# A decoder layer on one core: giving the maximum matmuls, turns and P.V places of their own in the written order

## The reference

```python
x = x + self_attention(layernorm(x))        # 16 heads of 16, 512 keys, two masked score entries
x = x + tanh(gate) * (cross_attention(layernorm(x), ctx) @ w_out + b_out)   # 16 heads of 64, 64 keys
h = layernorm(x)
a1, a2 = entmax15(layernorm_noaffine(h @ proj)) @ C1, ... @ C2     # 16 experts, rank 128
h = gelu(((([h, 1] @ Win1) * a1) @ Wout1.T))                       # 1024 wide
x = x + (([h, 1] @ Win2) * a2) @ Wout2.T
```

## Time and profile before

| | |
|---|---|
| median of 3 runs | 1161.67 us (1156.67 to 1162.15) |
| the profiled execution | 1160.25 us, span 1158.4 us |
| TensorE busy | 1042.9 us, 90% |
| VectorE, ScalarE, GpSimd busy | 768.1, 625.3, 150.2 us |
| mean granted clock of TensorE | 0.935 |

### The profile page before, as it was taken

The page is one execution under the profiler, slowest core; times in us unless marked ns, Lnnn a source line. Parts: engine busy times, 40 slices in busy tenths (PEclk is TensorE's granted clock), DMA queues, the critical chain, the costliest instruction groups (busy, mean ns, idle before and its releaser), DMA issues.

```text
span 1158.4 us, 16341 instructions
## 1 busy us (share of the span) xinstructions
PE 1042.9 (90%) x5310; PEld 598.8 (52%) x5310; DVE 768.1 (66%) x1575; ACT 625.3 (54%) x850; POOL 150.2 (13%) x174
## 2 busy tenths in 40 slices
PE   5898989889888999799989998999989997997977
PEld 4544333446444655465545654565546554655754
DVE  3574554677777867886687768786788577715762
ACT  2345655534554666465647474757556654664522
POOL 2000000012002210221011200220022102201311
PEclk9899988979996999999988999899989997998988
DMA  5677674721240142112411041104111310030001
GB/s 151 168 207 223 196 225 120 225 67 26 74 146 11 28 137 66 47 28 61 142 46 28 18 164 46 34 12 159 49 39 28 132 52 20 10 119 19 1 1 37
DMA packets 91288, 97.41 MB, mean 84 GB/s; under 512 B 10547, under 2 KB 76790, under 8 KB 89174
## 3 DMA queue, kind: packets, MB, share of 16 engines
q1 hardware_dynamic: 91222, 96.63, 28.2%
HBM read 41.34 MB, written 29.36 MB: 61 GB/s over the span
## 4 chain that ended last, share of the span: by engine, by line
PE 57%; DVE 18%; ACT 11%; issue 9%; DMA 3%; SPq 1%; POOL 1%; DVEq 0%; ACTq 0%
PE y_ps L758 17%; PE x_ps L758 13%; PE st_ps L758 9%; PE pv_ps L758 7%; PE sm_ps L758 5%; ACT probs L1190 3%; ACT L1190 3%; DVE mx L1390 2%; DVE cst L1480 2%; DVE cst L1473 2%; PE y_ps L905 2%; PE y_ps L872 1%; DMA xa<-in_x 1%; DMA a_scr<-a_cat 1%; ACT xt_hi L1190 1%
## 5 line engine op out<-in xcount | busy, mean ns | idle before, releaser
L1390 DVE TENSOR_REDUCE mx<-sm_ps 128x2 f32<-128x1024 f32 x256 | 312.7, 1222 | 170.2 <-PE sm_ps L758 161.5
L1190 ACT ACTIVATE probs<-st_ps 128x1024 f32<-128x1024 f32 x256 | 261.9, 1023 | 197.1 <-PE st_ps L758 196.0
L758 PE MATMUL st_ps<-q_st,k_st 52*128 52x512 f32 x512 | 206.9, 475 | 15.2 <-ACT probs L1190 13.5
L758 PE MATMUL sm_ps<-k_st,q_st 50*128 50x512 f32 x512 | 182.2, 478 | 6.6 <-DVE nm L1404 4.0
L758 PE MATMUL pv_ps<-probs,v_all 128*32 128x512 f32 x1024 | 148.3, 654 | 0.0
L758 PEld LDWEIGHTS st_ps<-q_st,k_st 52*128 52x128 f32 x512 | 84.2, 194 | 118.7 <-issue 68.5
L758 PE MATMUL x_ps<-b_cat,pt 128*128 128x256 f32 x448 | 114.7, 387 | 0.0
L758 PEld LDWEIGHTS x_ps<-b_cat,pt 128*128 128x128 f32 x448 | 78.4, 190 | 30.1 <-issue 18.4
L522 POOL TENSOR_TENSOR px<-px,cst 128x512 f32<-128x512 f32 x56 | 58.1, 1043 | 216.2 <-DVE cst L1485 216.1
L1190 ACT ACT_TABLE_LOAD x64 | 82.1, 1283 | 5.1 <-PE y_ps L758 3.2
L758 PEld LDWEIGHTS sm_ps<-k_st,q_st 50*128 50x128 f32 x512 | 70.7, 194 | 24.3 <-DVE mx L1390 12.1
(11 more groups left out here) (299 smaller groups left out, 1766.0 us busy)
## 6 DMA issues: line engine op xcount, KB each, us to landing
a_scr<-a_cat SPq DMA_DIRECT2D x32, 512.0 KB, 4.8
a_cat<-a_scr SPq DMA_DIRECT2D x8, 2048.0 KB, 8.1
q_st<-qk_hi SPq DMA_DIRECT2D x128, 64.0 KB, 2.3
k_st<-qk_hi SPq DMA_DIRECT2D x128, 64.0 KB, 2.3
b_scr<-b_cat SPq DMA_DIRECT2D x8, 1024.0 KB, 6.5
b_cat<-b_scr SPq DMA_DIRECT2D x8, 1024.0 KB, 9.7
xa<-in_x SPq DMA_DIRECT2D x9, 512.0 KB, 3.6
q_st<-qk_lo SPq DMA_DIRECT2D x64, 64.0 KB, 2.3
```

The costliest lines, as they stand in the source:

```text
L758: return nc.tensor.matmul(dst, lhs, rhs, start=start, stop=stop, **kw)
L1190: return nc.scalar.activation(dst, src, f, **kw)
L1390: nc.vector.tensor_reduce(mx[:, c % 2, :].rearrange("p (m x) -> p m x", m=2)[:, :, col], sm_ps[:], axis=AX, op=ALU.max).then_inc(sm_taken, 1)
```

## The change

The fixed parts become units of the tables: `M` (a pair of maximum matmuls, or its reduction), `TN` (the turn of the maxima), `PV` (P.V), while the score pair `P` stays fixed at each even tick in the loop. `scores` and `for_max` no longer stand by turns: a pair of scores is made together, a pair of maxima together. The loop's three tables are new. Setup with iterations 0 and 1 becomes one list for each engine (`EARLY_PE`, `EARLY_ACT`, `EARLY_DVE`) in which `P` and the setup units `SW` are entries too, and iteration 7 another (`LAST_*`); `TAIL_*` and `EARLY_SP` are written anew, the tail with five banks as before. In the lists the first number is the iteration `b`; dense and feed-forward kinds then act on `b-1`. No computation is added or left out.

```diff
 PE_TASKS = (
-    (10, "QK", 2, 0), (10, "QK", 2, 1), (12, "QK", 3, 0), (12, "QK", 3, 1), (12, "OT", 2, 0), (14, "OT", 3, 0),
-    (14, "Y", 1, 0), (14, "ON", 0, 0), (14, "ON", 1, 0), (17, "WO", 0, 0), (18, "WO", 0, 1), (18, "WO", 1, 0),
-    (18, "WO", 1, 1), (18, "AT", 0, 0), (18, "G", 0, 0), (20, "G", 1, 0), (22, "X2", 0, 0), (22, "X2", 1, 0),
-    (24, "H", 0, 0), (24, "H", 1, 0), (26, "S", 0, 0), (26, "S", 0, 1), (26, "S", 1, 0), (26, "S", 1, 1),
...
+    (12, "QK", 3, 1), (14, "OT", 2, 0), (14, "OT", 3, 0), (14, "M", 6, 0), (14, "Y", 0, 0), (14, "ON", 0, 0),
+    (14, "M", 7, 0), (16, "PV", 2, 0), (16, "M", 8, 0), (16, "Y", 1, 0), (16, "ON", 1, 0), (16, "TN", 1, 0),
+    (16, "PV", 3, 0), (16, "M", 9, 0), (18, "AT", 0, 0), (18, "WO", 0, 0), (18, "M", 10, 0), (18, "WO", 0, 1),
+    (18, "G", 0, 0), (18, "M", 11, 0), (18, "WO", 1, 0), (18, "WO", 1, 1), (20, "G", 1, 0), (22, "PV", 4, 0),
+    (22, "M", 12, 0), (24, "H", 0, 0), (26, "M", 13, 0), (26, "PV", 5, 0), (26, "X2", 0, 0), (26, "X2", 1, 0),
+    (26, "M", 14, 0), (26, "H", 1, 0), (26, "M", 15, 0), (26, "S", 0, 0), (26, "S", 0, 1), (26, "S", 1, 0),
...
+    (48, "ZM", 0, 0), (48, "M", 23, 0), (50, "PV", 11, 0), (50, "M", 24, 0), (52, "ZM", 1, 0), (52, "ZM", 2, 0),
+    (52, "TN", 3, 0), (52, "H", 6, 0), (52, "ZM", 3, 0), (52, "M", 25, 0), (52, "X3", 0, 0), (52, "X3", 1, 0),
...
 DVE_TASKS = (
-    (12, "OT", 3), (12, "Y", 1), (14, "LN1S", 1), (16, "LN1S", 2), (17, "ON", 0), (17, "ON", 1), (17, "EN", 4),
-    (17, "LN1S", 3), (17, "EN", 5), (18, "EN", 6), (18, "WO", 0), (18, "LN2S", 0), (18, "LN2S", 1), (18, "WO", 1),
...
+    (4, "EN", 2), (4, "EN", 3), (4, "QK", 0), (6, "M", 3), (6, "EN", 4), (6, "QK", 1), (8, "M", 4), (8, "OT", 0),
+    (8, "EN", 5), (8, "QK", 2), (8, "OT", 1), (8, "EN", 6), (10, "M", 5), (10, "QK", 3), (10, "OT", 2), (10, "OT", 3),
+    (12, "M", 6), (12, "Y", 0), (14, "M", 7), (14, "ON", 0), (16, "M", 8), (16, "Y", 1), (16, "TN", 1), (16, "ON", 1),
...
+LAST_DVE = (
...
+    (7, "LN3A", 2), (7, "LN3A", 3), (7, "X3", 0), (7, "X3", 1), (7, "EN", 0), (8, "EN", 1), (8, "EN", 2),
+    (8, "EN", 3), (8, "EN", 4), (8, "EN", 5))
...
 TAIL_PE = (
+    (8, "PJ", 0, 2), (8, "PJ", 0, 3), (8, "ZM", 3, 0), (8, "ZM", 4, 0), (8, "H", 5, 0), (8, "H", 6, 0),
+    (8, "ZM", 5, 0), (8, "H", 7, 0), (8, "ZM", 6, 0), (8, "ZM", 7, 0), (8, "Z1", 0, 0), (9, "Y", 0, 0),
+    (9, "Y", 1, 0), (9, "AT", 0, 0), (8, "Z1", 1, 0), (9, "G", 0, 0), (9, "G", 1, 0), (9, "H", 0, 0), (9, "H", 1, 0),
...
@@ block.tensor
+            def score_pair(b, t):
+                for r in (t % 4, t % 4 + 1):
+                    scores(b, t // 16, t // 4 % 4, r)
+
+            def max_pair(b, j):
+                c, i, r0 = j // 8, j // 2 % 4, 2 * (j % 2)
+                for r in (r0, r0 + 1):
+                    if c < 2:
+                        for_max(b, c + 2, i, r)
+                    else:
+                        for_max(b + 1, c - 2, i, r)
...
-            def iteration(b, project=True, setup_from=None):
-                for t in range(0, TICKS, 2):
-                    c, i, r0 = t // 16, t // 4 % 4, t % 4
-                    for r in (r0, r0 + 1):
-                        scores(b, c, i, r)
-                        if c < 2:
-                            for_max(b, c + 2, i, r)
-                        elif project:
-                            for_max(b + 1, c - 2, i, r)
-                    if r0 == 0:
-                        if t > 0:
-                            values(b, (t - 4) // 16, (t - 4) // 4 % 4)
-                        elif not is_first(b):
-                            values(b + -1, CH - 1, TT - 1)
-                    dense(b + -1, t, project, not is_first(b))
...
+            def iteration(b):
+                for t in range(TICKS):
+                    if t % 2 == 0:
+                        score_pair(b, t)
+                    for tick, kind, i, part in PE_TASKS:
+                        if tick == t:
+                            emit(b, kind, i, part)
```

More of the change, by code:

```diff
@@ L404, in plan, with in_tail, in_last, before_last @@
             return [u for u in PLAN if active(g, u[1])]
-        def in_tail(g):
-            return g.reg is None and g.off >= LAST
+        def in_tail(g, kind, i):
+            return g.reg is None and (g.off, kind, i) in TAIL_UNITS
+        def in_last(g, kind, i):
+            return g.reg is None and (g.off, kind, i) in LAST_UNITS
+        def before_last():
+            return SETUP_UNITS + sum(len(plan(At(None, k))) for k in range(LAST - 1))
         def before_tail():
-            return SETUP_UNITS + sum(len(plan(At(None, k))) for k in range(LAST))
+            return before_last() + len(LAST_UNITS)
         def order(g, kind, i):
-            if in_tail(g):
+            if in_tail(g, kind, i):
                 return before_tail() + TAIL_UNITS.index((g.off, kind, i))
+            if in_last(g, kind, i):
+                return before_last() + LAST_UNITS.index((g.off, kind, i))
             if g.reg is None and g.off == 0:
@@ L422, in order @@
             return SETUP_UNITS + before + len(PLAN) * (g.off - 2) + n
-        early = []
-        for t in range(SECOND_TICKS + TICKS):
-            early += [u[1:3] for u in plan(At(None, 0)) if u[0] == t - SECOND_TICKS]
-            early += [u[1:3] for u in SETUP_PE if u[0] == t]
+        early = [(u[0], u[2]) if u[1] == "SW" else u[1:3] for u in EARLY_PE if u[1] not in X_BANK and u[3] == 0]
         def setup_no(p, n):
@@ L510, in ln_passed @@
             count = 0
-            for u in TAIL_DVE:
-                if u[0] == LAST and u[1] in (f"LN{n + 1}S", f"LN{n + 1}M"):
+            for u in LAST_DVE + TAIL_DVE:
+                if u[0] == LAST + 1 and u[1] in (f"LN{n + 1}S", f"LN{n + 1}M"):
                     count += 1 if u[1][-1] == "S" else 2
-                if u == (LAST, kind, i):
+                if u == (LAST + 1, kind, i):
                     return 8 * LAST + count
@@ L977, in down @@
                 if k == 0:
-                    pe.wait_ge(o_taken, At(None, LAST).times(4, 0) if in_tail(g) else g.times(4, 4))
+                    pe.wait_ge(o_taken, At(None, LAST).times(4, 0) if g.reg is None and g.off >= LAST else g.times(4, 4))
                     wait(pe, z2_taken, g.times(1, -1))
@@ L989, in result, with emit @@
                 last.then_inc(y_full, 1)
[L991 to L995, removed]
-                    if kind in PROJECT:
-                        if project and kind == "X1":
-                            turn_x1(g + 2, i)
-                        if project and kind == "QK":
-                            qk(g + 2, i, (part,))
-                        continue
-                    if not body or not active(g, kind, i):
-                        continue
-                    task(g, kind, i, part)
+            def emit(b, kind, i, part):
+                if kind == "P":
+                    score_pair(b, i)
+                elif kind == "M":
+                    max_pair(b, i)
+                elif kind == "TN":
+                    turn_max(*((b, i + 1) if i < CH - 1 else (b + 1, 0)))
+                elif kind == "PV":
+                    if i == CH * TT - 1:
+                        values(b + -1, CH - 1, TT - 1)
+                    else:
+                        s = min(i, CH * TT - 1)
+                        values(b, s // TT, s % TT)
+                elif kind == "X1":
+                    turn_x1(b + 1, i)
+                elif kind == "QK":
+                    qk(b + 1, i, (part,))
+                elif active(b + -1, kind, i):
+                    task(b + -1, kind, i, part)
             def task(g, kind, i, part):
@@ L1167, in _ @@
             pe.wait_ge(rows_in, 16 * 12)
-            for t in range(0, SETUP_TICKS, 2):
-                for r in (t % 4, t % 4 + 1):
-                    for_max(first, t // 16, t // 4 % 4, r)
-                setup(t)
-                if t == 16:
-                    turn_max(first, 0)
-                setup(t + 1)
-            iteration(first, setup_from=SETUP_TICKS)
-            iteration(At(None, 1), setup_from=SECOND_TICKS)
+            for b, kind, i, part in EARLY_PE:
+                if kind == "SW" and b < 0:
+                    setup_ctx(i)
+                elif kind == "SW":
+                    setup_unit(b, i)
+                else:
+                    emit(At(None, b), kind, i, part)
             iteration(At(None, 2))
@@ L1179, in _ @@
                 iteration(At(it, 0))
-            iteration(At(None, B - 1), project=False)
-            for go, kind, i, part in TAIL_PE:
-                task(At(None, go), kind, i, part)
+            for b, kind, i, part in LAST_PE:
+                emit(At(None, b), kind, i, part)
+            for b, kind, i, part in TAIL_PE:
+                emit(At(None, b), kind, i, part)
         @block.scalar
@@ L1229, in qk_hi_part, with emit @@
                 run(qk_hi[:, j, :], qk_bank(a, j), ACT.Identity, bias=bqkv[:, j:j + 1]).then_inc(qk_hi_done, 1)
[L1231 to L1249 removed]
```

(67 more changed lines are left out.)

138 lines of the change are left out of this document (44 added, 94 removed), and 330 rows, old and new, of tables (ACT_TASKS, DVE_TASKS, EARLY_ACT, EARLY_DVE).

## The result

The changed kernel takes 1088.98 us (1085.39 to 1093.92, 4 runs), against 1161.91 us of the kernel before on the same chip: ratio 0.9397, interval 0.9352 to 0.9441, 73 us less. The forecast was 1131.5 us; the range ended at 1100. The profiled execution took 1085.39 us.

The account below looks back on a forecast made before the run. TensorE's own work was taken as the bound. Loop -7.5, setup and first iterations -9, last iteration and ending -13.5 sum to -30 us: 1160.25 to 1130.2, plus 1.4 for the runs' median, 1131.5 us; range 1100 to 1163.

Parts of the forecast that it names:

- an order can win only its idle time: Whole kernel: reordering wins only TensorE's idle time (about 8 us an iteration), low-clock time (up to 3.9) and the ending's waits.
- 8 x 0.39 = +3.1 for the splits: Loop: 8 more unbroken runs of score and maximum pairs an iteration, each costing TensorE 0.39 us, add 3.1 us.
- part 2: Loop's order, 5 iterations: waits -2.1, clock -2.5, splits +3.1, so -1.5 us an iteration, -7.5 us net.
- part 3: Setup and first two iterations: 6 us of waits, 3 of clock, 4 of idle time won, splits +3.9; -9 us net.
- part 4: Last iteration and ending: entmax moved earlier, waits gone, work put into the ending's idle time, clock kept; -13.5 us net.
- the five places found by walking both lists: Loop: new waits of 0.2 to 0.8 us at `M` 7, 13, 15, second `WO` and first `S`, 2 us in all.
- part 1: Own places for maxima: 53 more runs of score and maximum pairs at 0.39 us, +21 us over the kernel.
- the rounds through `a_cat` stay: First iteration: only 4 of 12 us idle time is won, as rounds through `a_cat` and the weights' DMAs stay.
- Waits nearly go and the clock stays: Rival, much faster: loop iterations of 118.8 us, loop -24, early -15, ending -17, giving 1106 us; chance 0.20.
- The "slower" rival: Splits and list order eat the gain: 0.6 us a split, 5 us of new waits an iteration, 1174 us; chance 0.17.
- the marks set for "right": Loop: `xt_lo` waits at most 1 us, idle under 7, clock 0.97 or more; ending some 95 us, no 6 us `zbuf` wait.
- those set for "wrong": More waits of `sm_ps` for `mx`; an iteration with 8 us idle and more busy time; loop clock under 0.94.

Follow-up runs that it names:

- old_all: Kernel before with only the pairing changed: both scores together, then both maxima, all orders old; 1149.66 us, ratio 0.9904.
- experiment 5: Needless matmuls put into TensorE's waits in the five middle iterations of `old_all`: 1154.45 us with those ahead of `WO`, 1147.34 us with those ahead of `AT` too.
- after_m_old: Changed kernel with the loop's maximum matmuls M 0 to 15 back at their old ticks on TensorE, four maxima moved on VectorE; 1195.07 us, ratio 1.029.
- after_merge: Changed kernel with the maxima put ahead of P.V where P.V stood between scores and maxima; 1108.88 us, ratio 0.9562.
- old_clock2: `old_all` with 8 needless matmuls ahead of the first `WO` and 8 ahead of `AT` in the five middle iterations; 1147.34 us, ratio 0.9902.

## Why the prediction was wrong

The direction, the bound (TensorE's own work) and the place of the gains were right, and the chosen case failed by size: -30 us forecast, -75 measured.

**The step that failed is that "an order can win only its idle time", the clock and the ending's waits, and with it the term "8 x 0.39 = +3.1 for the splits".** The waits came out nearly as summed. What was wrong is TensorE's busy time, which was to rise with the splits and fell. One iteration of before and two of after at the same granted clock, and one of after at 1.00:

```profile
443.60:564.70 121.10, 112.73 (x612) 65.53 (x609) 92.03 (x188) 73.33 (x95) 17.81 (x15) 0.99 0.22 67
...
410.90:528.40 117.50, 112.04 (x612) 65.66 (x609) 91.67 (x189) 73.36 (x95) 17.55 (x16) 0.99 0.23 69
528.40:647.10 118.70, 112.42 (x612) 65.75 (x609) 91.42 (x189) 73.42 (x95) 17.60 (x16) 0.99 0.22 67
647.10:764.10 117.00, 110.83 (x612) 64.54 (x608) 91.26 (x189) 73.29 (x95) 17.56 (x16) 1.00 0.22 68
```

The first is the kernel before, the others the changed one. The terms of part 2, in us an iteration:

```
                      forecast   measured
waits (idle time)         -2.1   -2.5 at a clock of 0.99, -2.4 with 1.00 after
busy time, no clock       +3.1   -0.5                     -2.0
clock                     -2.5   -2.8                     -1.4
sum                       -1.5   -5.8                     -5.8
```

The left column of the measured ones compares iteration 3 of before (121.1) with the mean of 3 and 4 of after (118.1), the right one with that of 5 and 6 (116.7); the clock is what is then left of 123.5 - 117.7, the means of all five. Either way the busy time is 3.6 to 5.1 us an iteration under the forecast, 18 to 26 us over the loop, whose whole miss is 22 us. It is the same over the whole kernel: TensorE's idle time fell by 32 us, where the prediction's waits add up to some 34 (10.5 in the loop, 10 in part 3, 13 with a share of clock in part 4; measured 10.4, 13.2 and 8.6). The busy time fell by 42.6 us, where 21 for splits and -17 for clock were to leave it about as it was.

The waits: over five iterations those for `ON`'s `xt_lo` (10.4 us) and for `res` (4.4) went, that for `probs` fell only from 6.1 to 3.8 (all 1.1 an iteration were to go), and several short ones shrank: about 25 us, 5.0 an iteration, where 3.0 + 1.1 + 1.0 were forecast. New ones did come, about 2.6 us an iteration where 3.0 were forecast: `qk_lo` 0.9 to 3.4 over the loop, `xt_f` 0.5 to 2.5, the other `xt_lo` 1.8 to 4.1, `mx` 1.4 to 3.5, `x1t_lo` 0 to 2.1, `zbuf` 0 to 1.5. So the sum was right and most of the places were not: three of the five places found by walking both lists were waits for `mx` (M 7, 13 and 15), and in the iteration shown above there is one such wait, of 0.4 us. That the two sums agree is in part luck. A tick in one engine's list says nothing of when another engine comes to it; ten maxima in TensorE's ticks 14 to 26 are VectorE's ticks 12 to 30.

Why the busy time fell is shown in part. The pairs alone took 0.8 us off it (112.7 to 111.9 in iteration 3 of `old_all`, same clock), for which the prediction had no term. The new order then changed it by +0.3 at a clock of 0.99, or by -1.2 with 1.00 after, in spite of 8 more splits. For that, sums from each start to the next, by what the matmul is, for iteration 3 of before (clock 0.99) and 5 of after (1.00):

```
                               before   after
scores and maxima                25.4    28.3
WO                                4.8     3.4
turns of the maxima, AT           4.0     0.8
ON, X2, X3, OT                    6.9     5.2
H                                 8.5     7.1
O (cross-attention, b_cat)       14.9    14.0
the rest                         56.6    58.2
sum                             121.1   117.0
```

Of the +2.9 of scores and maxima 2.6 are listed idle time behind them. The -0.9 of `O` holds no idle time: 8 of its matmuls stood ahead of a score pair before and 4 now. `WO`, `H` and the turns fell by more than the listed waits there. The profile counts 0.40 us for a matmul whose successor can start after 0.23 us, so it takes stops shorter than 0.17 us, and the first 0.17 of every longer one, for busy time; the iteration of before has 15 listed waits, that of after 10. That such hidden stops make up the rest is argued, not shown.

**The splits (part 1)** were counted right: 32 unbroken runs an iteration before, 40 after, 273 and 325 in all (52 more, 53 forecast). By distances between starts the price of 0.39 holds with full-width work on both sides: 0.1 for the change on each side, and 0.42 for a lone pair where a pair in a group takes 0.33, which is 2 x 0.42 - 0.66 = 0.18 more. Beside P.V only the 0.17 are left, as P.V's successor starts 0.52 us behind its last matmul whatever it is. In the loop the changes between half-height pairs and full-width work other than P.V grow from 47 to 56 and 16 pairs stand alone: by these prices an estimate of 0.9 + 16 x 0.09 = +2.3 us an iteration, forecast +3.1. What the splits cost in the loop was not measured apart; whatever it was, most of it or more was offset elsewhere in the busy time. The rule of the Trainium skill weighed in the forecast ("TensorEngine Tiling (Array Packing)", Tiling Modes (Key Properties): a change of tiling mode drains TensorE) agrees with the 0.1 us on either side; that every split costs so, which was my step from it, doesn't hold beside P.V.

**The clock** in the loop is not where the forecast failed: -2.5 us an iteration, and -1.4 to -2.8 measured, by the reference taken. But granted clock and waits aren't two sums to be added: from iteration 3 to 4 of the kernel before the clock falls from 0.99 to 0.95, busy time rises by 3.8 us, idle time falls by 0.6, and the iteration is 3.2 longer. Outside the loop the time "lost" fell by 31.5 us; at the 2.9 us for 5.0 of experiment 5 that is worth some 18 us (an estimate), where the prediction had 4.5 and a share of another 4.5.

**The pairs** were credited with the 1.1 us an iteration of waits for `probs`, against 1 us of new waits. Alone they gave 11 us over the whole kernel. The second score no longer stands 0.33 us behind the first, so each exponential starts that much sooner; in the second iteration the waits for `probs` fell from 4.8 to 3.2 us by this alone, while those for `mx` rose from 1.5 to 2.7 (the maxima start 0.33 us later). That the earlier exponential is the cause of the 11 us is argued from this, not tried apart.

**Setup and first iterations (part 3)**: -9 forecast, -26 measured. The waits of the second iteration could be read from the trace of before, 12.3 us in all; 6 were taken off, and those for `probs`, the largest, have no term in part 3. In the kernel before, from 203.03 to 318.47 us:

```profile
PE st_ps L758 <- ACT probs L1190: 4.8, 4, 1.3
PE y_ps L758 <- DVE xt_lo L1624: 2.0, 1, 2.0
PE sm_ps L758 <- DVE mx L1390: 1.5, 2, 1.2
PE y_ps L872 <- DVE xn L1454: 1.2, 1, 1.2
```

and in the changed kernel, from 193.55 to 292.20:

```profile
PE st_ps L913 <- ACT probs L1336: 1.3, 2, 1.1
PE y_ps L1040 <- DVE xn L1567: 0.8, 2, 0.6
```

9.4 us of idle time went (forecast 6), and the time "lost" to the low clock fell by 7.4 us (forecast 3 us of time). Busy time fell by 7.4 us, 2 of them the moved projection matmuls, where the splits were to add to it. In iteration 0 the waits behind `a_cat`, 5.9 us, went to 0.2, which "the rounds through `a_cat` stay" had excluded; the wait for a weight's DMA stayed (3.1 and 1.5 before, 4.2 after). The first 80 us are least certain: the four kernels with the same early list took 77.6 to 80.1 us there, at granted clocks from 0.91 to 0.96.

**Last iteration and ending (part 4)** came nearest: -13.5 forecast, -19.3 measured, -16 with these lists alone. Where TensorE waited 5.97 us for `zbuf` there is no wait now; the two for `zbuf` that are left in the ending are 0.9 and 0.8 us. The last iteration gave more than forecast (-14.9, its clock went from 0.93 to 1.00), the ending less: it has a wait of 3.4 us, at 1000.83 us, for which the profile names no releaser and which the kernel before had not.

**The rivals.** "Waits nearly go and the clock stays" (0.20, 1106 us) came nearest, with another mix: in the loop it had 115.8 us busy and 3 idle in an iteration, measured are 111.5 and 6.1; and it had -15 for the early part. The "slower" rival is what `after_m_old` became (1195 us): one list out of step with the other, and the sign turns. How much the match of the lists gives, no row of before could price.

Of the marks set for "right", the waits for `xt_lo` (0.8), idle time under 7 us (5.5 to 7.0), the loop's clock (0.97 to 1.00) and `zbuf` hold; from the last P.V to the end it is 99 us, where some 95 were the mark (105 before). Of those set for "wrong" one did show: the maximum matmuls waited 3.2 us over the loop for `mx`, where in the kernel before only the turns did (1.4).

What stays open: what offset the splits in the busy time of the new order, and whether the low clock at 457 to 463 and 577 to 583 us of the changed kernel (0.68, 0.75, 0.60 and 0.84 in four stretches of 3 us) has a cause in this order. No wait of over 0.9 us stands close ahead there, but several short ones do: TensorE was busy 2.00 of 3 us from 451.2 and 1.52 of 3 us from 574.2. Neither was tried.

## What to carry to other kernels

When work between in-order engines is reordered, follow each producer and consumer through both lists in order; positions in different lists are not times, and a new wait that one list seems to make may be the one the other list was written around. Give the busy time of the bounding engine a term that can fall, too: here the idle time was forecast within 0.4 us an iteration and the busy time missed by 3.6 to 5.1, since neighbours in the order and stops too short to be listed are in it. Cost every stage from its own view of waits, the first iterations too, and don't add clock and waits as if apart. Where lists are made to match, a part can be worth nothing or less: moving VectorE's part alone gave nothing here, and undoing one part of the matched lists cost 20 to 106 us.

## What the runs showed of the hardware

- The granted clock isn't set by the idle time of an iteration alone. `after_merge` idles 8.8 to 9.2 us an iteration in iterations 3 to 6, in waits of at most 1.1 us, at a clock of 0.99 to 1.00. `old_all` idles 8.2 to 9.3 us there, at 0.99 in the two iterations with one wait of 2.1 us, and at 0.97 and 0.95 in the two that have another of 2.0 us. In `old_clock2`, with both filled, it is 0.97 to 1.00.
- What a lower granted clock costs is no fixed share of length times one minus the clock. `old_all`'s iteration 5 at 0.95 (6.2 us by that count) took 2.9 us longer than `old_clock2`'s at 0.99 (1.2); 0.99 against 1.00 cost 0.1 us or nothing between these two kernels, and 1.4 us between iterations 3, 4 and 5, 6 of the changed kernel (118.1 and 116.7). Each is one profiled execution.
- P.V's eight 32-column matmuls are followed at 0.52 us at the soonest by anything, half-height pairs too, so it is the one neighbour that takes a change of height for nothing on that side.
